# Cross-attention walked in halves of the context: one slot is one head over 1024 rows instead of two heads over 512

## The reference, cut to what matters

```python
    x = x + _L0_xattn_ref(_layernorm(x, axis=-1), ctx_768, ...)
...
        q = (x @ Wq).reshape(B, Nq, HEADS, DIM_HEAD)
        k = (context @ Wk).reshape(B, context.shape[1], HEADS, DIM_HEAD)
        v = (context @ Wv).reshape(B, context.shape[1], HEADS, DIM_HEAD)
        sim = jnp.einsum('bihd,bjhd->bhij', q, k) * SCALE
        attn = jax.nn.softmax(sim, axis=-1)
        out = jnp.einsum('bhij,bjhd->bihd', attn, v)
```

## Time and profile before

| | before |
|---|---|
| median of 3 runs | 918.85 us (918.46 to 920.45) |
| span of the profiled execution | 917.6 us |
| PE busy | 903.4 us, 98% |
| ACT busy | 628.3 us, 68% |
| DVE busy | 590.5 us, 64% |
| POOL busy | 504.8 us, 55% |
| granted clock of PE | 1.000 |

### The profile page before, as it was taken

How to read it: one execution, slowest core, us unless ns; L and a number is a source line. 1 busy time by engine, 2 the same in 40 slices (tenths; PEclk the granted TensorE clock), 3 DMA queues, 4 the chain that set the end, 5 groups by cost and what they waited for, 6 DMA issues and landing times.

```text
span 917.6 us, 20100 instructions
## 1 busy us (share of the span) xinstructions
PE 903.4 (98%) x7470; PEld 564.5 (62%) x7470; DVE 590.5 (64%) x1069; ACT 628.3 (68%) x1398; POOL 504.8 (55%) x393
## 2 busy tenths in 40 slices
PE   6999999999999999999999999999999999999998
PEld 3556666666666666666666666666666455544444
DVE  6546666656666666666666666666667769886634
ACT  4857887777788788788878778877776523235540
POOL 4637656566556666666665655787777755310000
PEclk9999999999999999999999999999999999999999
DMA  9478677876767677677677868967999662333502
GB/s 333 98 142 167 135 129 141 163 145 139 136 142 131 135 146 138 132 137 141 134 143 152 157 130 140 194 133 146 186 190 165 105 133 64 72 86 74 183 13 80
DMA packets 340271, 126.38 MB, mean 138 GB/s; under 512 B 316113, under 2 KB 317905, under 8 KB 340177
## 3 DMA queue, kind: packets, MB, share of 16 engines
q1 hardware_dynamic: 325232, 96.66, 57.0%
q10 hardware_dynamic: 14944, 28.45, 9.6%
HBM read 45.36 MB, written 2.10 MB: 52 GB/s over the span
## 4 chain that ended last, share of the span: by engine, by line
PE 90%; DVE 3%; ACT 2%; SPq 2%; DMA 1%; issue 1%; ACTq 0%; DVEq 0%
PE v_ps L658 28%; PE k_ps L658 26%; PE e_ps L727 9%; PE e_ps L658 8%; PE o_ps L749 6%; PE o_ps L752 3%; PE e_ps L1014 3%; PE o_ps L1007 1%; PE e_ps L1007 1%; PE o_ps L768 1%; DMA raw<-in_ctx_t 1%; PE o_ps L947 1%; PE v_ps L1007 1%; DVE q_max L1531 1%; SPq L624 1%
## 5 line engine op out<-in xcount | busy, mean ns | idle before, releaser
L1984 POOL TENSOR_TENSOR p_l<-p_f,p_h 128x1024 f16<-128x1024 f32 x128 | 272.4, 2128 | 237.3 <-ACT p_f L1195 237.3
L1190 ACT ACTIVATE p_h<-e_ps,bias 128x512 f16<-128x512 f32 x256 | 175.7, 686 | 2.6 <-issue 0.5
L1195 ACT ACTIVATE p_f<-e_ps,bias 128x512 f32<-128x512 f32 x256 | 176.4, 689 | 0.0
L1526 DVE TENSOR_TENSOR k_l<-k_ps,k_h 128x512 f16<-128x512 f32 x128 | 88.5, 691 | 132.3 <-ACT k_h L1160 132.3
L1518 DVE TENSOR_TENSOR v<-v_ps,v 128x512 f16<-128x512 f32 x127 | 87.5, 689 | 107.0 <-ACT v L1152 107.0
L1531 DVE TENSOR_REDUCE q_max<-e_ps 128x2 f32<-128x1024 f32 x128 | 150.8, 1219 | 8.0 <-PE e_ps L727 0.9
L658 PE MATMUL v_ps<-wv_h,ctx_h 128*128 128x256 f16 x756 | 124.4, 273 | 1.2 <-DVE v L1518 1.1
L658 PE MATMUL v_ps<-wv_l,ctx_h 128*128 128x256 f16 x756 | 123.7, 273 | 0.0
L658 PE MATMUL v_ps<-wv_h,ctx_l 128*128 128x256 f16 x756 | 123.7, 273 | 0.0
L749 PE MATMUL o_ps<-v,pt_h 128*128 128x128 f16 x1024 | 104.2, 220 | 0.5 <-issue 0.5
L658 PE MATMUL k_ps<-ctx_h,wk_h 128*128 128x512 f16 x384 | 103.8, 379 | 0.0
(11 more groups left out here) (311 smaller groups left out, 1399.0 us busy)
## 6 DMA issues: line engine op xcount, KB each, us to landing
raw<-in_ctx_t ACTq DMA_DIRECT2D x26, 768.0 KB, 5.3
w_raw<-in_w_t SPq DMA_DIRECT2D x32, 256.0 KB, 3.8
raw<-in_ctx_t SPq DMA_DIRECT2D x5, 768.0 KB, 7.0
pt_h<-p_h SPq DMA_TRANSPOSE x128, 3.7
pt_l<-p_l SPq DMA_TRANSPOSE x128, 3.3
out<-xr SPq DMA_DIRECT2D x7, 256.0 KB, 2.0
x_in<-in_x SPq DMA_DIRECT2D x6, 256.0 KB, 11.0
o_all<-in_x ACTq DMA_DIRECT2D x6, 256.0 KB, 3.5
```

What stands on the lines that cost most here:

```text
L1190: act.activation(p_h[:, s % H_RING, h, :], e_ps[s % 2][:, h, :], ACT.Exp, scale=EXP_SCALE, bias=bias[:, n % 2, h, q:q + 1]).then_inc(p_hi, 1)
L1195: act.activation(p_f[:, s % F_RING, h, :], e_ps[s % 2][:, h, :], ACT.Exp, scale=EXP_SCALE, bias=bias[:, n % 2, h, q:q + 1], accum_out=p_su ...
L1526: dve.tensor_tensor(k_l[:, n % 2, cols], k_ps[:, :], k_h[:, n % 2, cols], ALU.subtract).then_inc(k_split, 1)
L1984: pool.tensor_tensor(p_l[:, s % L_RING, :, :], p_f[:, s % F_RING, :, :], p_h[:, s % H_RING, :, :], ALU.subtract).then_inc(p_split, 1)
```

## The change

The order of the slots and their shape change. Each batch is walked in two halves of 1024 context rows, and each half over all four pairs. A slot is now **one head over 1024 rows**: 16 slots a batch as before, the first 8 for the first half and the last 8 for the second. Two slots (the two heads of a pair, one half) are a unit. Keys are made for a unit (a ring of 4 units), and the scores of a unit are one step that fills both `e_ps`, head 0 in the one and head 1 in the other, and starts when the exponentials of the whole unit before are done.

Per slot the two heads' exponentials of 512 columns become one instruction of 1024 for `p_h` and one for `p_f`. The maximum is one number a slot. In a second-half slot (`behind(s)`: `s % 16 >= 8`) DVE combines its maximum with that of the first half in one more instruction, `new_max` (L1542), before ACT may make the bias. So the second half needs no fade of its own, and the first half's `acc` and row sum are faded once, when the second half comes. `stage_low`, `fade_sums` and the first quarter's scaling go. The matmuls are the same in number and shape.

Around it: the order of the first context and weight pieces changes on ACT, DVE and SP (`wv_high(1)` moves from round 2 to round 1, `ctx_high(2)` from before the queries to round 1, `wv_low(1)` and `wk_low` to rounds 1 to 3). At the end both score slots stand before `fold(0)`.

```diff
-                pe.wait_ge(k_split, s + 1)
-                if s >= 2:
-                    pe.wait_ge(p_full, 2 * s - 2)
...
+                b, _, p, _ = slot_of(2 * u)
+                pe.wait_ge(k_split, 2 * u + 2)
+                if u:
+                    pe.wait_ge(p_full, 2 * u)
...
+                for i in range(2):
+                    cols = slice(i * QW, i * QW + QW)
+                    for left, right, first, last in ((q_h, k_h, True, False), (q_h, k_l, False, False), (q_l, k_h, False, True)):
+                        for h, rows in enumerate(head_rows):
+                            mm = pe.matmul(e_ps[h][:, i, :], left[rows, p, tokens], right[rows, u % K_RING, cols],
+                                           start=first, stop=last)
                 mm.then_inc(e_filled, 1)
...
             weighted_values(SLOTS - PV_LAG)
-            scores(SLOTS - 2)
+            scores(UNITS - 1)
             fold(0)
-            scores(SLOTS - 1)
             project_out(0)
...
+            def slot_maximum(s):
+
+                col, old = s % PER_BATCH, s % PER_BATCH - PER_HALF
+                dve.wait_ge(e_filled, s // 2 + 1)
+                ins = dve.tensor_reduce(q_max[:, col:col + 1], e_ps[s % 2][:, :, :].rearrange("p i n -> p (i n)"), AX, ALU.max,
+                                        negate=True)
+                if behind(s):
+                    ins.then_inc(e_reduced, 1)
+                    dve.wait_ge(e_reduced, s // PER_BATCH * PER_HALF + s % PER_HALF + 1)
+                    ins = dve.tensor_tensor(new_max[:, col:col + 1], q_max[:, col:col + 1], q_max[:, old:old + 1], ALU.min)
+                ins.then_inc(e_maxed, 1)
...
+            def add_sums(s):
+                b, _, p, h = slot_of(s)
+                col, old = s % PER_BATCH, s % PER_BATCH - PER_HALF
+                dve.wait_ge(p_full, s + 1)
+                dve.wait_ge(fade_ready, PER_HALF * b + s % PER_HALF + 1)
+                dve.scalar_tensor_tensor(o_den[:, p, h, :], p_sum[:, old:old + 1], fade[:, col:col + 1], p_sum[:, col:col + 1],
+                                         ALU.mult, ALU.add).then_inc(o_rec_ready, 1)
...
+                act.activation(p_h[:, s % H_RING, :, :], e_ps[s % 2][:, :, :], ACT.Exp, scale=EXP_SCALE,
+                               bias=bias[:, col:col + 1]).then_inc(p_hi, 1)
...
+                act.activation(p_f[:, s % F_RING, :, :], e_ps[s % 2][:, :, :], ACT.Exp, scale=EXP_SCALE,
+                               bias=bias[:, col:col + 1], accum_out=p_sum[:, col:col + 1]).then_inc(p_full, 1)
...
                 if ahead:
                     if pair:
-                        quarter_bias(x)
-                    exps(x, 0)
+                        slot_bias(x)
+                    exps_high(x)
                     if pair:
-                        quarter_bias(x + 1)
+                        slot_bias(x + 1)
                 if 0 < s and s + 1 < SLOTS:
                     v_high(s + 1)
...
                 if ahead:
-                    exps(x, 1)
+                    exps_full(x)
                 if 0 < s < SLOTS:
                     k_high(s)
-                if ahead and pair and (x + 1) % QUARTERS == 3:
-                    fade_of(x // QUARTERS)
+                if ahead and behind(x):
+                    fade_of(x)
```

More of the change, by code:

```diff
@@ L72, in perceiver_kernel @@
         ("c_sum", [P, B], F32), ("c_col", [P, B], F32),
-        ("p_sum", [P, 2, 2, QUARTERS], F32), ("p_faded", [P, 2, QUARTERS], F32), ("o_den", [P, 2, 1], F32), ("shift", [P, 4], F32),
+        ("p_sum", [P, PER_BATCH], F32), ("o_den", [P, PAIRS, 2, 1], F32), ("shift", [P, 4], F32),
     ])
@@ L158, in perceiver_kernel @@
     assert t_halves_end <= halves_end
-    (o_all, ident, causal, bo_row, bv_row, b2_row, bq_col, bk_col, b1_col, b2_half, stats, mean_var, rstd, exponent,
-     q_max, bias, low, fade, acc, o_rec, o_sum, o_f,
+    (o_all, ident, causal, bo_row, bv_row, b2_row, bq_col, bk_col, b1_col, stats, mean_var, rstd, exponent,
+     q_max, bias, new_max, fade, acc, o_rec, o_sum, o_f,
      ones, bq_half, bk_half, bias_prod, u_col, w_col, w_half, s_col, c_sum, c_col,
-     p_sum, p_faded, o_den, shift) = keep.values()
+     p_sum, o_den, shift) = keep.values()
     q_h, q_l = queries.values()
@@ L723, in scores @@
                     pe.wait_ge(xt_split, 4)
[L724 to L728, removed]
+                tokens = slice(b * T, b * T + T)
+                for i in range(2):
[4 more added lines that the diff above has]
+                                           start=first, stop=last)
                 mm.then_inc(e_filled, 1)
             def weighted_values(s):
-                n, q = stage_of(s)
-                b, p = pair_of(n)
+                b, half, p, h = slot_of(s)
                 g = p // 2
@@ L744, in weighted_values @@
                     pe.wait_ge(q_split, 8)
[L745 to L754, removed]
+                acc_bank, head = o_ps[s % 2], 2 * (p % 2) + h
+                for j in range(2 * JT):
+                    tile = 2 * JT * half + j
+                    pe.matmul(acc_bank[:, 0:VW], pt_h[:, s % T_RING, j, :], v[g][:, tile, head, :],
+                              start=(j == 0), stop=False, skip_group_check=True)
+                    mm = pe.matmul(acc_bank[:, 0:DH], pt_l[:, s % T_RING, j, :], v[g][:, tile, head, 0:DH],
+                                   start=False, stop=(j == 2 * JT - 1), skip_group_check=True)
                 mm.then_inc(pv_done, 1)
@@ L815, in steady @@
                     weighted_values(s - PV_LAG)
-                if s % 2 == 0 and 2 <= s <= SLOTS:
-                    scores(s - 2)
-                    scores(s - 1)
+                if s % 2 == 0 and 2 <= s < SLOTS:
+                    scores(s // 2 - 1)
             for s in range(1, SLOTS):
@@ L1538, in accumulate @@
             def accumulate(s):
-                n, q = stage_of(s)
+                b, half, p, h = slot_of(s)
+                col = s % PER_BATCH
                 dve.wait_ge(pv_done, s + 1)
-                if q == 0:
-                    dve.wait_ge(fade_ready, n + 1)
-                    if n >= 2:
-                        dve.wait_ge(o_ready, n - 1)
-                else:
-                    dve.wait_ge(acc_ready, s)
-                for h in range(2):
-                    new, total = o_ps[s % 2][:, h * VW:h * VW + VW], acc[:, n % 2, h, :]
-                    faded = fade[:, n % 2, h, q:q + 1]
-                    if q == 0:
-                        ins = dve.tensor_scalar(total, new, faded, None, ALU.mult)
-                    else:
-                        ins = dve.scalar_tensor_tensor(total, new, faded, total, ALU.mult, ALU.add)
@@ L2064, in _ @@
                 done = s - PV_LAG - 1
-                if done >= 0 and done % QUARTERS == 3:
-                    o_norm(done // QUARTERS)
+                if done >= 0 and stage_end(done) is not None:
+                    o_norm(stage_end(done))
                 for r in ADD_BIAS.get(s, ()):
@@ L2089, in norm_low @@
                 pool.tensor_tensor(n_half[:, r, 1, :], o_all[:, norm_at(what, r), :], n_half[:, r, 0, :], ALU.subtract).then_inc(nh_split, 1)
-            for r in range(3):
-                inverse_deviation(r)
+            inverse_deviation(0)
+            inverse_deviation(1)
+            o_norm(STAGES - 2)
+            inverse_deviation(2)
             for r in range(3):
```

219 lines of the change are left out of this document (104 added, 115 removed).

## The result

The changed kernel takes **949.54 us** (median of 4 runs, 947.76 to 951.63), the kernel before 918.84 (918.46 to 920.45) beside it: ratio 1.0334, interval 1.0317 to 1.0351. The profiled execution spans 947.7 us, 30.1 more than before. Forecast were 947.7 us and a range of 941 to 958.

A forecast was written before the change was run, and what follows sets the result against it. PE was taken to bound the kernel, busy 903.4 of 917.6 us. `new_max` against POOL 25.0, the end 3.0 and the start 0.8 summed to 28.8 us: 946.4 on the span, 947.7 predicted, range 941 to 958.

The forecast's parts named there:

- PE bounds, and its matmuls stay: Whole run: PE is busy 903.4 of 917.6 us; lighter ACT or DVE can bring back no more than some 2 us.
- `new_max` waits for POOL's two-input instruction: Second-half rounds with context to split: DVE's `new_max` stands until POOL's `ctx_l` ends, delaying PE; together 25.0 us.
- the lock doesn't bite: Rival: `new_max` slips in or POOL's instruction has moved away, leaving 3.0 + 0.8, so 922.7 us; chance 0.08.
- Not slower: Rival: ACT's lighter slots free the rounds and the end's loss is made up, 917.5 us; chance 0.03.
- Its size: Loss per held round: 1.54 us, 1.73 with `fade_of` ahead of `ctx_h`, 2.18 in batch 6.
- The total, and where it was luck: Whole kernel: 25.0 + 3.0 + 0.8 = 28.8 us lost, 946.4 on the profiled span, 947.7 as median.
- How often: 14 held rounds: six of each kind in batches 0 to 5, two in batch 6; round 108 adds about 1.0 us.
- Ordinary second halves keep up: Second-half rounds: `v_low` ends at 308.02, PE may go at 308.16 with 0.15 us left; cost nothing, bound 0.3 a round.
- longer chain: Rival: 0.45 us more in the chain makes 17 other pairs miss by 0.3 each, 959.1 us; chance 0.11.
- The end: Last scores: both slots wait for `p_f` of slot 125 with nothing else queued on PE; 3.0 us, bounds 1.5 and 4.
- The start: Before slot 3's `v_high` on ACT: `wv_h` and a `ctx_h` stand ahead, first maximum later; 0.8 us, between 0 and 2.5.
- The page's rule: Rival: any POOL SBUF read blocks two-input DVE, so `weight_high` also stops `new_max` in four rounds; 948.8 us, chance 0.06.

The follow-up runs named there:

- run 8: Changed kernel with `new_max` as `tensor_scalar`, `fold(0)` and its splits moved ahead at the end, and `ctx_high(2)` back ahead of slot 0's exponentials: 920.04 us.
- run 1: Changed kernel with `new_max` made by `tensor_scalar`, the old maximum as scalar pointer, in place of two SBUF tensors: 924.39 us.
- run 2: Kernel before, with an unused one-column `tensor_tensor` of two SBUF inputs behind each maximum of second-half slots, releasing ACT's bias: 942.27 us.
- run 3: Kernel before, with the unused one-column instruction behind second-half maxima as `tensor_scalar` with a scalar pointer: 919.36 us.
- run 4: Changed kernel with POOL's `ctx_low` written as two instructions of 768 columns instead of one of 1536: 931.21 us.
- run 7: Changed kernel with `fold(0)` ahead of the last scores on PE, and its splits ahead of slot 126's work on ACT and DVE: 946.52 us.
- run 5: Changed kernel with POOL's `weight_high` as a two-input `tensor_tensor` adding `raw` to itself, leaving out the weights' scale: 950.96 us in one run.
- run 6: Changed kernel with `fold(0)` ahead of the last unit's scores on PE alone: 949.79 us.

## Why the prediction was right, step by step

- **PE bounds, and its matmuls stay.** Right. ACT became 52.9 us lighter and nothing came of it: with the new stalls taken away (run 8) the time is that of before.
- **`new_max` waits for POOL's two-input instruction.** Right, and shown from four sides: run 1 takes it away, run 2 puts it into the kernel before, run 3 is its control, run 4 shortens it. The rival "the lock doesn't bite" (922.7) is out in the changed kernel; run 1, where it can't bite, shows about its time, 924.4. "Not slower" (917.5) is out too.
- **Its size.** Right to within a tenth for the 12 ordinary ones. The sum was of time lost between value tiles and the next value tiles. That step is 4.60 us where nothing holds (368.80 to 373.40), as before, and 6.10, 6.28 (379.49 to 385.77) and 7.20 in the held rounds: 1.50, 1.68 and 2.60 lost. From the last go 0.58 that the kernel before loses there too (its step is 5.18), which leaves 2.02. The sum had 1.54, 1.73 and 2.18. PE's waits in the profile (1.34, 1.52, 2.44) are each 0.16 less than the time lost, because they are counted from the modelled end of the matmul before. From the end of `new_max` to PE's start it is 2.93 us (382.84 to 385.77), where the sum had 2.92. The exponential takes 1.11 to 1.12 as forecast (1.13).
- **The total, and where it was luck.** Without the fall of the clock the loop costs 23.7 us (run 7's profile), not 25.0, and the whole change 27.1 on the span where the sum had 28.8. Two clock falls, which no term priced, add 3.0 and make it 30.1. So the sum came within 1.3 us of the span, with an error of 1.7 one way (the loop 1.3 and what follows the end 0.5 less, the start 0.1 more) and 3.0 the other. The median is 1.8 above the forecast: 1.3 of it is this, 0.5 that it lies 1.8 above the profiled span and not 1.3.
- **How often.** Six long ones of each kind in batches 0 to 5, as predicted; in batch 6 two of 2.91 us at 623.91 and 648.63 and the 1.07 beside `add_bias` at 637.19, which lost PE 0.76 (predicted about 1.0; the step is 5.36). PE has no wait for `v` in a first half but the start's own two, 1.53 and 0.15, which the count of 17 contains.
- **Ordinary second halves keep up.** Right: 0.16 at 370.17, no wait of PE. `v_low` ends at 373.11, 4.31 after the value tiles at 368.80, and the sum had 4.31 as well (308.02 less 303.71), with 0.15 left. The rival "longer chain" (959.1) needed 0.45 more in it; run 1 added 54 ns to each `new_max`, 0.11 a pair, without a wait.
- **The end.** The last scores start 7.10 us after the last keys (736.99 to 744.09) and before 4.12 (710.81 to 714.93), 2.98 lost where the sum had 3.0. But the end cost 4.4: 1.4 of clock were missing from that term. I had written that a clock below 1.000 would make the prediction wrong altogether; it did fall (0.996 over the span), which cost 3 us in all, and the range held it.
- **The start.** 0.9 against 0.8. Run 8 removes it with `ctx_high(2)` in its old place; that run has run 1's remedy too, which alone leaves the value tiles at 58.53, so most of it is the place of `ctx_high(2)`. The 1.53 us that PE waited for `v` at 42.63 is gone there; 0.46 for `ctx_l` at 41.88 stands in its place.
- **The page's rule** (the Trainium skill, SBUF — State Buffer, section "SBUF: two separate sides") counts any GpSimd instruction that reads SBUF. The trace disagrees for `TENSOR_SCALAR` (0.16 us at 717.00, inside 715.70 to 718.75) and agrees for `TENSOR_TENSOR` in the very same place (0.63 in run 5). That the later one is blocked until the other's instruction ends agrees with 380.85, where `new_max` ends with `ctx_l`. No run here looks at POOL waiting for DVE.

## What to carry to other kernels

Before a small DVE instruction with two tensors in SBUF goes into a chain that others wait for, look at what POOL does at that moment; a column of one number a partition can stand 3 us behind a wide instruction. If one operand is a column, give it as the scalar pointer: 25 us for one line here. And when a step is moved earlier on the engine that bounds, move what empties its bank on the other engines too, or the wait only changes its name (run 6 against run 7).

## What the runs showed of the hardware

- DVE stood for a POOL instruction only when both read two tensors from SBUF, for the forms tried: 0.214 and 0.204 us for DVE's `TENSOR_SCALAR` beside POOL's `ctx_l`, 0.69 as always for DVE's `TENSOR_TENSOR` with one tensor from PSUM beside POOL's `p_l`, 0.16 for DVE's `TENSOR_TENSOR` beside POOL's `TENSOR_SCALAR`, up to 2.91 for two and two.
- The wait ends with POOL's instruction, even if another stands right behind it: longest 1.45 with `ctx_l` in halves.
- PE's clock fell to its 1.2 GHz level behind waits of 2.44 to 2.87 us. Behind the 2.85 to 2.87 us before the last scores it fell in all four profiles that have it (the changed kernel, runs 1, 4 and 5); behind the two of 2.44 it fell at 655 in the changed kernel and run 6, at 629.6 in run 5, at neither in run 7. It fell behind none of the waits of 1.2 to 1.7 us. In the changed kernel it cost 1.4 us in the end and 1.6 in the loop, in run 1 it cost 2.7 in the end.
